# Three of thirteen row one-hot columns of each group made by ScalarE instead of VectorE

## What is computed

```python
h  = layernorm(x)
msg = silu(concat(h[src], h[dst], d2) @ mW1 + mb1)      # per edge
msg = silu(layernorm(msg) * g + b @ mW2 + mb2)          # shortened
agg = segment_sum(msg, src, 3125)
x   = x + h + (silu(concat(h, agg) @ uW1 + ub1) @ uW2 + ub2)
x   = x + ffn_on_the_top_half_of_rows(layernorm(x))
```

## Time and profile before

| what | us |
|---|---|
| median of 3 runs (2434.20 to 2435.62) | 2434.29 |
| the profiled execution: device time | 2433.59 |
| the profiled execution: span, first to last instruction | 2431.8 |

### The profile page before, as it was taken

The page is one execution under the profiler, slowest core; times in us unless marked ns, Lnnn a source line. Parts: engine busy times, 40 slices in busy tenths (PEclk is TensorE's granted clock), DMA queues, the critical chain, the costliest instruction groups (busy, mean ns, idle before and its releaser), DMA issues. The chain is left out here.

```text
span 2431.8 us, 52303 instructions
## 1 busy us (share of the span) xinstructions
PE 2062.2 (85%) x11942; PEld 1721.6 (71%) x11943; DVE 2045.6 (84%) x6836; ACT 1373.9 (56%) x2906; POOL 1133.5 (47%) x1096
## 2 busy tenths in 40 slices
PE   2432566439999999999999999999999999668998
PEld 1221455338888888888888888888888888555776
DVE  7998999949989999999999999999999998264970
ACT  0004111038777778777877777777787877122231
POOL 7654355455555555555554555555555552242010
PEclk9999788559999999999999999999999999888999
DMA  3000000032222222222222222222222221301000
GB/s 115 0 0 0 21 27 26 13 106 73 72 68 72 72 70 72 72 71 71 72 72 68 71 71 72 72 69 71 73 72 69 71 72 34 88 0 26 1 30 23
DMA packets 65763, 134.99 MB, mean 56 GB/s; under 512 B 20958, under 2 KB 36309, under 8 KB 65464
## 3 DMA queue, kind: packets, MB, share of 16 engines
q0 software_dynamic: 42016, 111.40, 16.1%
q1 hardware_dynamic: 22435, 22.18, 3.0%
q10 hardware_dynamic: 1266, 0.83, 0.1%
HBM read 124.20 MB, written 10.16 MB: 55 GB/s over the span
## 5 line engine op out<-in xcount | busy, mean ns | idle before, releaser
L836 POOL DMA_INDIRECT g_rows<-b_table,idx_pair x834 | 790.8, 948 | 745.7 <-DVE idx_pair L977 567.8
L947 PE MATMUL ps<-w2g,nT 128*128 128x256 f32 x3336 | 790.1, 380 | 0.0
L947 PEld LDWEIGHTS ps<-w2g,nT 128*128 128x128 f32 x3336 | 602.2, 191 | 64.8
L862 ACT ACTIVATE normed<-act,shift,rstd_e 128x255 f32<-128x255 f32 x834 | 452.2, 592 | 137.3 <-DVE shift L1049 136.3
L986 DVE TENSOR_TENSOR agg<-psG,agg 125x256 f32 x834 | 349.3, 419 | 125.3 <-issue 61.2
L930 PE MATMUL psG<-msg,ohf 128*125 128x256 f32 x1668 | 427.6, 379 | 0.0
L883 ACT ACTIVATE nT<-psM 128x512 f32<-128x512 f32 x417 | 248.4, 596 | 124.3 <-PE psM L939 85.3
L1092 DVE BATCH_NORM_STATS2 stat_e<-act 128x6 f32<-128x256 f32 x834 | 311.8, 418 | 0.0
L921 PE MATMUL psH<-a_sb,ohT 128*128 x1668 | 303.9, 304 | 0.0
L930 PEld LDWEIGHTS psG<-msg,ohf 128*125 128x125 f32 x1668 | 283.5, 187 | 24.6 <-ACT msg L879 0.2
L1085 DVE TENSOR_TENSOR g_rows<-psH,g_rows 128x512 f32<-128x512 f32 x417 | 287.4, 689 | 15.3 <-remote 6.4
(11 more groups left out here) (202 smaller groups left out, 2625.5 us busy)
## 6 DMA issues: line engine op xcount, KB each, us to landing
g_rows<-b_table,idx_pair POOLq DMA_INDIRECT x834
h_sb<-in_x SPq DMA_DIRECT2D x1, 3125.0 KB
b_table<-b_out SPq DMA_DIRECT2D x25, 125.0 KB
x_sb<-in_x SPq DMA_DIRECT2D x1, 3125.0 KB
out<-x_sb SPq DMA_DIRECT2D x5, 625.0 KB
rec_d<-rec SPq DMA_DIRECT2D x1, 1668.0 KB, 7.8
agg<-rec_d SPq DMA_DIRECT2D x6, 256.0 KB, 3.5
row<-score_d SPq DMA_DIRECT2D x1, 1525.9 KB
```

The source lines that it names most:

```text
L836: pool.indirect_dma_start(g_rows[:, j, n, :], None, b_table[:, :], bass.IndirectOffsetOnAxis(ap=idx_pair[:, j, n:n + 1], axis=0)).then_inc ...
L862: ins = nc.scalar.activation(normed[:, (j - 9) % 2, n, 0:D - 1], act1[:, (j - 9) % RING, n, 0:D - 1], ACT.Identity, scale=rstd_e[:, 1 - fa ...
L947: mm = pe.matmul(ps2[:, k, n, :], nT[:, k, n, q, :], w2g[:, q, :], start=(q == 0), stop=(q == 1))
```

## The change

The row one-hot of a group is split. DVE makes columns 0 to 9 as before, as one instruction of 1280 elements in place of 1664. Columns 10 to 12 (`ACOLS = 3`) are made by ACT in a new function `row_marks(s)`: three activations, one a column, give `(iota - r)^2` with the bias `-r` from a per-partition operand (`neg_r`, made once by one more DVE instruction over 806 columns; it lies in `f1`), into a bf16 buffer in the space of `f2`; a fourth activation over 384 elements gives `relu(1 - 2 * square)`, which is 1 where the two are equal and 0 elsewhere. `route(s)` waits for both parts. ACT runs `row_marks(0)` ahead of the loop and `row_marks(s + 1)` as the first thing of round `s`.

```diff
+                def row_marks(s):
+                    if s >= 2:
+                        act.wait_ge(s_win, s - 1)
+                    if s:
+                        act.wait_ge(s_ora, s)
+                    for k in range(ACOLS):
+                        c = (s + 1) * COLS - ACOLS + k
+                        nc.scalar.activation(apart2[:, k, :], iota_n[:, :], ACT.Square,
+                                             bias=neg_r[:, c:c + 1]).then_inc(s_square, 1)
+                    act.wait_ge(s_square, (s + 1) * ACOLS)
+                    nc.scalar.activation(or_[:, s % 2, COLS - ACOLS:COLS, :], apart2[:, :, :], ACT.Relu,
+                                         scale=-2.0, bias=1.0).then_inc(s_ora, 1)
+
+                act.wait_ge(s_negr, 1)
+                row_marks(0)
                 for s in range(SUPERS):
                     b = s // 2
+                    if s + 1 < SUPERS:
+                        row_marks(s + 1)
                     if s % 2 == 0 and b < BLOCKS:
                         turned(b)
...
                 def route(s):
                     pe.wait_ge(s_or, s + 1)
+                    pe.wait_ge(s_ora, s + 1)
...
+                dve.wait_ge(s_loc, 1)
+                V.tensor_scalar(neg_r[:, :], f2[:, :], -1.0 / WIN, None, ALU.mult).then_inc(s_negr, 1)
...
-                    V.tensor_tensor(or_[:, s % 2, :, :], r_all[:, own].unsqueeze(2).broadcast_to([P, COLS, P]),
-                                    iota_n[:, :].unsqueeze(1).broadcast_to([P, COLS, P]), ALU.is_equal)
+                    mine = slice(s * COLS, (s + 1) * COLS - ACOLS)
+                    V.tensor_tensor(or_[:, s % 2, 0:COLS - ACOLS, :],
+                                    r_all[:, mine].unsqueeze(2).broadcast_to([P, COLS - ACOLS, P]),
+                                    iota_n[:, :].unsqueeze(1).broadcast_to([P, COLS - ACOLS, P]), ALU.is_equal)
```

More of the change, by code:

```diff
@@ L35 @@
 LEAD = 2
+ACOLS = 3
 EQR = 4
@@ L140, in build @@
             tb_i = sb("tb_i", [P, TG], I32)
+            neg_r = f1
+            apart2 = f2[:, 0:ACOLS * P // 2].bitcast(BF16).rearrange("p (t r) -> p t r", t=ACOLS)
             or_ = sb("or_", [P, 2, COLS, P], BF16)
@@ L216, in build @@
             s_or = sem("s_or")
+            s_negr = sem("s_negr")
+            s_square = sem("s_square")
+            s_ora = sem("s_ora")
             s_win = sem("s_win")
```

## The result

| kernel | median us | runs | ratio to before |
|---|---|---|---|
| before | 2434.36 | 4 (2434.20 to 2435.62) | |
| the change | 2491.20 | 4 (2487.50 to 2496.94) | 1.0234, interval 1.0211 to 1.0258 |

The change costs 57 us, 2.3%. The direction was forecast, the size was not: 2456 was predicted, with 2482 as the upper end. The profiled execution took 2487.50 us, with a span of 2485.8.

The account below looks back on a forecast made before the run. DVE was taken to bound the kernel before, the ACT-PE loop of waits after. Start +4.0, groups 9 to 49 +17.4 and tail +0.6 made +22.0 us, hence 2456 us; range 2441 to 2482.

Parts of the forecast that it names:

- The ring and its place: ACT-PE loop of waits, `hT` to next `hT`: 5.73 us a pair before, 8.53 with two `row_marks` calls, becoming the bound.
- The marks: One `row_marks` call on ACT, three Squares and a Relu: 1.40 us, bounds 1.05 and 1.75.
- DVE's part: Row one-hot on DVE, 1280 elements instead of 1664: 0.39 us less a group, 6.88 us a pair if DVE bound.
- PE's part of the ring: From start of `hT` to the even group's copy, PE's tables, next turn and routing: mean 4.90 us, present clock, chance 0.70.
- Rival 4: PE's clock falls: every pair like the slow one, 6.09 us, loop of waits 9.72, +46 us, 2480; chance 0.15.
- The start: Up to the copy of group 9: three early sets of marks delay it, partly won back, +4.0 us.
- The tail: From the copy of group 49 to SP's read: ACT's DMA wait delays `windows(56)`, scatters catch up, +0.6 us in all.
- Rivals 1 and 2: ACT's idle time takes the marks, DVE stays bound; or POOL's scatters bound and gain: faster, 2423 us; together 0.07.
- rival 2: POOL's scatters bound and gain from shorter DVE work, down to 4.82 us a pair; 0.07 shared with ACT's-idle-time rival.

Follow-up runs that it names:

- The marks without a reader: Kernel before plus ACT's marks in the change's places, written to a buffer nobody reads, DVE still making all thirteen columns: 2497.37 us, ratio 1.0244.

## Why the prediction was right in kind and wrong in size

- **The ring and its place: right.** The parts of it that are ACT's own came out as worked out: 0.15, 0.53, 0.15, and DVE waits for the first table copy in nearly every pair, 3.45 us in the pair shown (some 2 were forecast, with the shorter ring). The marks without a reader show that nothing else of the change is needed for the loss. DVE's share of the loop fell to 66%, not to about 80%, since the pair was longer than forecast.
- **The marks: right.** 1.43 us a set against 1.40. A Square took 0.392 (0.38 forecast) and the Relu of 384 elements 0.522 (0.48):

```profile
L327 ACT ACTIVATE f<-iota_n,f x186: 384/392/412, 239.1 to 536.2; 128x128 bf16<-128x128 bf16 x186
L330 ACT ACTIVATE or_<-f x62: 522/522/523, 240.1 to 536.6; 128x384 bf16<-128x384 bf16 x62
```

- **DVE's part: right.** The shorter one-hot took 1.482 us (1.49 forecast).
- **PE's part of the ring: wrong, and this is the step that failed.** I took 4.90 us, the mean of four pairs before the change, "ring at about the present clock 0.70". Measured: 6.51 on the mean of 20 pairs. The difference, 1.6 us times 20 pairs, is 32 of the 33 us missing in that stretch; the rest is the marks, 0.06 us a pair. The four pairs were not a poor sample (all 20 of before have 4.85): the step that failed is carrying their mean, and the clock in it, over to a loop with other pauses. Before the change PE paused 0.61 us ahead of each `hT` and longer (2.85 us in one pair) ahead of the odd routing, where it waited for DVE. Now all of the pause, 3.5 us, stands ahead of `hT`, and the higher clock fell into it. Adding matmuls into that pause brought PE's part to 3.65 and the clock to 1.00: so the low clock is what made PE's part long, and the pause is what the clock went with. How the chip decides is not shown by these runs.
- **Rival 4 was this mechanism,** and had 0.15. Its price was too low as well: 2480, with 6.09 us as the slowest pair of before. In that pair the last part of PE's work had more of the higher clock: the two routings took 1.54 us for 26 matmuls, in the changed kernel 1.90.

```profile
399.77 1.54 PE L568 MATMUL psK<-oqv,or_ 128*128 128x96 bf16 x26
```

  At the lower clock up to the copy it is 6.54, and 20 x (6.54 + 0.83 + 2.86 - 7.66) = +51 is what was measured. The range ended at a pair seen before, not at the price of the lower clock throughout. The sign that the prediction gave for this rival (a pair well above 9, a mean clock below 0.75) is what came: 10.19 us and 0.67.
- **The start: a little low.** +4.17 at the copy of group 1 (4.2 forecast), but +4.45 at the first scatter (3.4 forecast) and +5.5 at group 9 (4.0): the ring already binds in most of groups 2 to 9 (pairs of 8.72 and 9.00 us, with the clock at 0.72 between 249.3 and 292.6 us). That `neg_r` costs nothing held: the first `hT` came 2.79 later, two sets of marks and no more.
- **The tail: right in its steps.** It came out at -0.8 in place of +0.6. `windows(56)` started 24.92 after the copy of group 49 (25.15 forecast), after an idle time of 5.56 on DVE (about 6 forecast):

```profile
521.30 1.49 DVE L728 TENSOR_TENSOR or_<-r_all,iota_n 128x1280 bf16<-128x1280 f32 x1 [5.56 <-PE psK L592]
```

  The scatters lagged 6.9 us behind the last `oqv` in place of 9.4; I had taken some 8.1.
- **Rivals 1 and 2** fell. ACT's idle time could have taken the marks, but only in another place of its program; there it did. The scatters don't bound the change (POOL waits 111 us for ACT), but they do bound the tail of the faster versions, as rival 2 said for the case without the ring.

## What to carry to other kernels

Idle time on an engine is not room for work wherever it is put: find the ring of waits that runs through it, and place new work behind the instruction that starts the other engine, not ahead of it. When PE is in the ring, price its part at both clock levels, and don't carry over the mean of before: a longer pause may take the clock, and then every pair pays. Where two bounds are close and one of them varies from pair to pair, setting mean against mean can mislead, and so can taking the longer in each pair. With one column the pair took 7.96 us, where the first way gives 7.40 and the second 7.78, because a wait in one pair made the next one late. With the marks behind the copies it took 6.83, DVE's own length, where the second way would give 7.2, because the longer and the shorter pairs evened out. Follow two or three pairs in a row, with what each passes on to the next.

## What the hardware showed that was not expected

- PE can be given its higher clock just while it is mostly idle: 1.00 over 3.40 us with 0.58 us of work, 0.50 over the 6.80 us before with 6.16 us of work, pair after pair, and on a second chip as well (1.00 with 0.55, 0.50 with 6.19 us of work).
- 19 blocks times four matmuls whose results are thrown away made the changed kernel 2.0% faster.
- The clock's pattern can repeat with the pairs for a long time: with three columns PE's part took 6.54 us in 15 pairs on end, with one column it went 3.65, 6.35, 5.33 over and over, and with PE kept busy 3.65 in 17 pairs on end. That the pair's length and the clock hold each other fast is a guess; with the marks that nobody reads the pattern broke for two pairs and came back.
- Between chips the kernel before differed by up to 0.9% (2438 and 2416 us). The two profiled executions of the change, 2487.50 and 2471.41 us, differ only behind the routing: from SP's read to the end they took 1938.4 and 1921.0 us, while the routing ended at 547.4 and 548.7.
